# Two-step expert kernel on one core: the low parts of state, velocity, shared and halt layer, and the residual sum of iteration one, on GpSimd instead of VectorE

## What is computed

```python
v = 0; integrated = x
for _ in range(2):
    ctx = concat(integrated, v)
    shared_ctrl = gelu(ctx @ w_s1 + b_s1) @ w_s2 + b_s2
    x_shared, v_shared = _inl(shared_ctrl, integrated, v, mu)   # alpha, beta, gate
    hidden = gelu(ctx @ w1[expert] + b1[expert])                # the two experts of the token
    ctrl = hidden @ w2[expert] + b2[expert]
    x_r, v_r = _inl(ctrl, integrated, v, mu), weighted over the two
    x_next = sw * x_shared + (1 - sw) * x_r
    v_next = sw * v_shared + (1 - sw) * v_r
    halt = sigmoid(gelu(x_next @ w_h1 + b_h1) @ w_h2 + b_h2)
    refined = gelu(x_next @ w_f1 + b_f1) @ w_f2 + b_f2
    integrated = integrated + halt * refined * integration_weight
    v = v_next
```

## Time and profile before

| | before |
|---|---|
| median of 3 runs | 372.2 us (371.07 to 373.6) |
| the profiled execution | 371.76 us, of it 370.0 us span |
| TensorE busy | 332.4 us (90%) |
| VectorE busy | 285.4 us (77%) |
| ScalarE busy | 196.3 us (53%) |
| GpSimd busy | 17.4 us (5%) |
| mean granted TensorE clock | 0.967 |

### The profile page before, as it was taken

One profiled execution on the slowest core, in us unless ns is written; L12 is line 12 of the kernel. 1 busy time (PEld: TensorE's weight loads), 2 busy tenths in 40 slices (PEclk: granted clock), 3 DMA queues, 4 the chain that ended last, 5 costly groups with the idle time before them and its releaser, 6 DMA issues.

```text
span 370.0 us, 4365 instructions
## 1 busy us (share of the span) xinstructions
PE 332.4 (90%) x1508; PEld 229.5 (62%) x1516; DVE 285.4 (77%) x596; ACT 196.3 (53%) x306; POOL 17.4 (5%) x20
## 2 busy tenths in 40 slices
PE   4989999899897696897999999999999999989943
PEld 4754985454565474575765776767767767756621
DVE  0648676565968769989889999999989988991942
ACT  3500053477372682468586866748467366356421
POOL 0030111211111102000000000000000000000000
PEclk9989999999999999699899999999999999999985
DMA  7999910000000000000000000000000000000000
GB/s 264 424 411 293 357 41 0 1 1 2 0 2 1 0 2 0 0 2 1 1 2 0 0 0 2 0 2 1 0 3 0 0 0 30 0 0 30 28 1 28
DMA packets 10725, 17.84 MB, mean 48 GB/s; under 512 B 336, under 2 KB 8528, under 8 KB 9424
## 3 DMA queue, kind: packets, MB, share of 16 engines
q1 hardware_dynamic: 10704, 17.57, 13.7%
HBM read 16.52 MB, written 1.05 MB: 47 GB/s over the span
## 4 chain that ended last, share of the span: by engine, by line
PE 70%; DVE 14%; issue 8%; ACT 3%; POOL 2%; DMA 2%; POOLq 1%; ACTq 0%; SPq 0%; DVEq 0%
PE ps L1124 66%; DVE zz L761 3%; DVE lst L746 2%; POOL lrs L347 2%; DMA ctxT<-in_ctxT 2%; PE ps L1221 1%; PE ps L1200 1%; ACT hid L467 1%; DVE st L646 1%; DVE lmv L749 1%; PE ps L1307 1%; DVE a L662 1%; POOLq L62 1%; PE ps L1295 0%; DVE lve L751 0%
## 5 line engine op out<-in xcount | busy, mean ns | idle before, releaser
L1124 PE MATMUL ps<-hm_odd,ew_hi 128*128 128x512 f32 (+1 forms) x169 | 52.6, 423 | 0.0
L1124 PE MATMUL ps<-hm_even,ew_hi 128*128 128x512 f32 (+1 forms) x160 | 49.2, 415 | 0.0
L1124 PEld LDWEIGHTS ps<-hm_odd,ew_hi 128*128 128x128 f32 (+1 forms) x169 | 28.4, 192 | 5.9
L1124 PEld LDWEIGHTS ps<-hm_even,ew_hi 128*128 128x128 f32 (+1 forms) x160 | 26.4, 189 | 5.1
L1124 PE MATMUL ps<-hm_odd,ew_lo 128*128 128x512 f32 (+1 forms) x80 | 27.8, 398 | 0.0
L1124 PE MATMUL ps<-hm_even,ew_lo 128*128 128x512 f32 (+1 forms) x80 | 27.4, 391 | 0.0
L467 ACT ACTIVATE hid<-ps,pB 128x512 f32<-128x512 f32 x32 | 21.7, 687 | 10.6 <-PE ps L1124 9.9
L1124 PE MATMUL ps<-x_hi,w1x_hi 128*128 128x512 f32 x40 | 19.9, 498 | 5.6 <-ACT hid L467 3.9
L761 DVE TENSOR_SCALAR zz<-ps,lmv,lrs 128x128 f32<-128x128 f32 x48 | 16.4, 405 | 7.7 <-POOL lrs L347 7.5
L855 DVE SCALAR_TENSOR_TENSOR ring<-ring,pB,hid 128x1024 f32<-128x1024 bf16 x16 | 20.5, 1282 | 0.9
L746 DVE BATCH_NORM_STATS2 lst<-ps 128x6 f32<-128x128 f32 x48 | 10.7, 286 | 11.9 <-PE ps L1200 11.8
(11 more groups left out here) (271 smaller groups left out, 750.4 us busy)
## 6 DMA issues: line engine op xcount, KB each, us to landing
ring<-in_fc1b SPq DMA_DIRECT2D x4, 1024.0 KB, 17.3
ring<-in_fc2a SPq DMA_DIRECT2D x4, 1024.0 KB, 9.9
packC<-in_packC SPq DMA_DIRECT2D x1, 1152.0 KB, 9.2
pB<-in_packB SPq DMA_DIRECT2D x1, 1109.5 KB, 10.0
ctxT<-in_ctxT SPq DMA_DIRECT2D x2, 512.0 KB, 6.4
xtok<-in_xtok SPq DMA_DIRECT2D x1, 1024.0 KB, 9.0
xT<-in_xT SPq DMA_DIRECT2D x1, 1024.0 KB, 11.0
a<-in_fc1a SPq DMA_DIRECT2D x1, 1024.0 KB, 13.0
```

The lines of the kernel that those rows point to most:

```text
L1124: return pe.matmul(out, lhsT, rhs, start=start, stop=stop)
```

## The change

Four pieces of VectorE's work move to GpSimd. `shared_low` is `shared_halves`, `state_low` is the part of `state_split` for steps 2 to 7 (for steps 0 and 1 the split stays on VectorE), `residual` is line 1081, and `halt_low` moves under its own name for steps 0 to 6; VectorE keeps its own `halt_low` and calls it once, for step 7. In numbers: 8 instructions on `hsh`, 6 on `x_lo`, 4 on `v_lo`, 4 on `xT` and 7 on `h1s`. VectorE's final sum now waits for GpSimd's residual (`xsum`). On GpSimd each of the new instructions is followed by a wait for its own semaphore.

```diff
--- before.py
+++ after.py
@@ -346,6 +346,51 @@
                 pool.wait_ge(sem("lve"), n + 1)
                 pool.tensor_tensor(lrs[:, n % 2, :], lve[:, n % 2, :], mhalf[:, 0:BPC], ALU.pow)\
                     .then_inc(sem("lrs"), 1)
+
+            def shared_low(s):
+
+                pool.wait_ge(sem("hs"), s + 1)
+                pool.wait_ge(sem("hsu"), s + 1)
+                pool.tensor_tensor(hsh[64:128, s % 2, :], hs[64:128, :], hsh[64:128, s % 2, :].bitcast(F),
+                                   ALU.subtract).then_inc(sem("hsl"), 1)
+                pool.wait_ge(sem("hsl"), s + 1)
+
+            def state_low(s):
+
+                c = s % NCH
+                pool.wait_ge(sem("hid_ps"), 5 * s)
+                pool.wait_ge(sem("xhi"), s + 1)
+                pool.tensor_tensor(x_lo, xi[:, ck(c)], x_hi.bitcast(F), ALU.subtract).then_inc(sem("xlo"), 1)
+                pool.wait_ge(sem("xlo"), s + 1)
+                if s >= NCH:
+                    pool.wait_ge(sem("vhi"), c + 1)
+                    pool.tensor_tensor(v_lo, vT[:, ck(c)], v_hi.bitcast(F), ALU.subtract).then_inc(sem("vlo"), 1)
+                    pool.wait_ge(sem("vlo"), c + 1)
+
+            def residual(s):
+
+                pool.wait_ge(sem("xi"), s + 1)
+                pool.tensor_tensor(xT[:, ck(s)], xT[:, ck(s)], xi[:, ck(s)], ALU.add).then_inc(sem("xsum"), 1)
+                pool.wait_ge(sem("xsum"), s + 1)
+
+            def halt_low(s):
+
+                pool.wait_ge(sem("h1"), s + 1)
+                pool.tensor_tensor(h1s[32:64, :], h1[32:64, :], h1s[32:64, :].bitcast(F), ALU.subtract)\
+                    .then_inc(sem("h1lo"), 1)
+                pool.wait_ge(sem("h1lo"), s + 1)
+
+            pool.wait_ge(sem("lrs"), 3 * NCH)
+            shared_low(0)
+            for s in range(STEPS):
+                if s + 1 < STEPS:
+                    shared_low(s + 1)
+                if 2 <= s < NCH + 2:
+                    residual(s - 2)
+                if s + 2 < STEPS:
+                    state_low(s + 2)
+                if s >= 1:
+                    halt_low(s - 1)
 
         @block.scalar
         def _(act):
@@ -881,35 +926,21 @@
                 c = s % NCH
                 if s >= 1:
                     dve.wait_ge(sem("hid_ps"), 5 * s)
-                if s < 2:
-                    dve.tensor_copy(x_hi, xi[:, ck(c)]).then_inc(sem("xhi"), 1)
+                dve.tensor_copy(x_hi, xi[:, ck(c)]).then_inc(sem("xhi"), 1)
                 dve.wait_ge(sem("xhi"), s + 1)
                 dve.tensor_tensor(x_lo, xi[:, ck(c)], x_hi.bitcast(F), ALU.subtract).then_inc(sem("xlo"), 1)
-                if s >= NCH:
-                    dve.wait_ge(sem("vhi"), c + 1)
-                    dve.tensor_tensor(v_lo, vT[:, ck(c)], v_hi.bitcast(F), ALU.subtract).then_inc(sem("vlo"), 1)
-
-            def hidden_masked(s, next_state):
+
+            def hidden_masked(s):
 
                 kept(s, 1)
                 if s == 1:
                     weigh(NCH - 2, 2)
                 kept(s, 2)
-                if next_state:
-                    state_split(s + 1)
                 lower(s, 0)
                 lower(s, 1)
                 kept(s, 3)
                 lower(s, 2)
-                shared_halves(s)
                 lower(s, 3)
-
-            def shared_halves(s):
-
-                dve.wait_ge(sem("hs"), s + 1)
-                dve.wait_ge(sem("hsu"), s + 1)
-                dve.tensor_tensor(hsh[64:128, s % 2, :], hs[64:128, :], hsh[64:128, s % 2, :].bitcast(F),
-                                  ALU.subtract).then_inc(sem("hsl"), 1)
 
             ln_stats("ffn", 0)
             ln_scale("ffn", 0)
@@ -1013,7 +1044,6 @@
             kept(0, 3)
             state_split(1)
             lower(0, 2)
-            shared_halves(0)
             lower(0, 3)
             route(NCH - 1)
             dve.wait_ge(sem("consts"), 4)
@@ -1077,9 +1107,8 @@
                 link(dve.scalar_tensor_tensor(rr, th, 1.0, rr, ALU.add, ALU.mult))
                 if s < NCH:
                     dve.tensor_tensor(xi[:, ck(c)], xi[:, ck(c)], rr, ALU.add).then_inc(sem("xi"), 1)
-                    dve.wait_ge(sem("xi"), s + 1)
-                    link(dve.tensor_tensor(xT[:, ck(c)], xT[:, ck(c)], xi[:, ck(c)], ALU.add))
                 else:
+                    dve.wait_ge(sem("xsum"), c + 1)
                     dve.tensor_tensor(res[:, ck(c)], xT[:, ck(c)], rr, ALU.add).then_inc(sem("res"), 1)
 
             def state_next_split(s):
@@ -1105,9 +1134,7 @@
                 if s >= 1:
                     state_next_split(s - 1)
                 if s + 1 < STEPS:
-                    hidden_masked(s + 1, s + 2 < STEPS)
-                if s >= 1:
-                    halt_low(s - 1)
+                    hidden_masked(s + 1)
                 if s == 0:
                     slot_masks(NCH - 1)
             stepped(STEPS - 1)
```

## The result

The changed kernel takes 376.0 us (median of four executions, 375.2 to 377.0) against 372.5 us (371.1 to 373.6) for the kernel before on the same chip: a ratio of 1.0088, with a 95% interval of 1.0065 to 1.0111. It is slower by 3.5 us; 379.3 was forecast. The profiled execution took 375.86 us (span 374.1); the one of before took 371.76 (span 370.0).

The account below looks back on a forecast made before the run. VectorE was taken to pace iterations 2 to 4; holds of 1.15 us, each replacing 0.69, summed to +7.06 us on 371.76 (378.8), plus half a microsecond for the clock: 379.3 us, range 370.0 to 387.

Parts of the forecast that it names:

- VectorE paces iterations 2 to 4: Step loop: TensorE waits for VectorE's `xn_lo`, so each moved instruction's effect on VectorE's time repeats in the kernel's time.
- GpSimd holds VectorE back: Shared SBUF path: a two-input GpSimd instruction keeps VectorE's next two-input or fast copy instruction out; chance 0.63 for at least 0.97 us.
- the rival without a hold: VectorE is not held and gets 3.45 us shorter per iteration; kernel 1.8 us faster, near 370.0 us; chance 0.18.
- The hold of 1.15 us: Each moved instruction blocks VectorE for GpSimd's assumed duration, 1.15 us, and saves 0.69: d = +0.46 us each.
- s = 2, 3, 4 late by 1.85 (2.2 less the slack of 0.36), 4.5 and 6.8 us: Hand-over of `xn_lo` to TensorE: VectorE late by +2.2, +4.5 and +6.8 us, TensorE's slack of 0.36 at s = 2.
- the formula 17d - 1.0: Lateness at s = 4 for any net cost d per moved instruction: seventeen instructions less pauses; 3.7 us for a 0.97 us hold.
- s = 5 and 6 absorb the rest: VectorE is 7.8 and 7.3 us late, but TensorE's slack of 1.0 and 1.6 us keeps it at +6.8.
- s = 7, +0.26 us more: At s = 7 VectorE loses two instructions (-1.38) and meets one hold (+1.15); TensorE was waiting, so +7.06 after +6.8.
- Tail 0: After s = 7: last `h1s` stays on VectorE; the one before comes some 0.6 us later, but hidden: 0.
- +0.5 us for TensorE's clock, between 0 and 1.7: Behind TensorE's stall at s = 4: a lower granted clock could cost up to 1.7 us; half a microsecond was added.
- GpSimd's order: GpSimd's strict queue: no TensorE wait expected for `h1s` or `x_lo`; a first one would add less than 1 us.
- Signs: If right: VectorE instructions beside GpSimd's take 1.8 us; s = 3 starts near 233, s = 4 near 259, idle 2 or more.

Follow-up runs that it names:

- the 18 early instructions: Of the change's 29 instructions only the 18 that GpSimd executes up to s = 4 move, the rest stay on VectorE: 377.5 us against 372.6, ratio 1.014.
- the 11 late ones: Only the other 11 of the change's instructions, from `x_lo` of step 6 on, go to GpSimd: 372.8 us, ratio 1.0007.
- The extra two-input instructions: Kernel before kept whole, plus 29 unused GpSimd subtractions of 512 columns, two SBUF inputs, where the moved ones run: 394.8 us against 372.7, ratio 1.059.
- the one-input experiment: Kernel before kept whole, plus 29 unused GpSimd copies of 512 columns with one SBUF input: 378.8 us against 372.7, ratio 1.016.
- the one with the changed kernel's split ahead: Changed kernel with VectorE's split into `xn_hi` and `xn_lo` placed ahead of `refine`, `xn_hi` in its own place: 375.3 us, ratio 1.0075.
- the deferred sums: Kernel before with the split ahead of `refine` and the four residual sums deferred to iterations 5 and 6, all on VectorE: 370.7 us, ratio 0.995.

## Why the prediction was right or wrong, point by point

- **VectorE paces iterations 2 to 4: right.** TensorE's new waits are where they were put (0.78, 1.77 and 1.85 us), all loss is made by the 18 early instructions (377.5 us against 372.8 for the 11 late ones), and an earlier `xn_lo` only moves the wait elsewhere.
- **GpSimd holds VectorE back: right.** The extra two-input instructions, whose result nobody reads, cost 22 us; the rival without a hold (370.0 us) is out. The row that decided, GpSimd's 0.97 us of waiting at 139.98, had its mirror image in `xn_lo`. (Of line 855 1.11 us were left at that moment and not 0.97; nothing hangs on it.)
- **The hold of 1.15 us: the term that failed.** It was set equal to GpSimd's own duration, and that was put between two reads one after the other (0.95) and two reads and a write (1.37). Both steps were off. The instruction alone takes 1.26 us and not 1.15, and it holds VectorE for less than it lasts: 0.95 us on `xn_lo`, 0.98 over an iteration. The rate of the earlier trace rows gives 0.95 for two reads as well, but as far as the runs show that is chance: one read would by it be half of that, and 0.28 to 0.33 us was measured. The prediction had a better value in hand: for 0.97 us, the one wait between the two engines then on record, it gives 3.7 us at s = 4. By the estimate from the Trainium skill that the prediction named (GPSIMD Engine Reference, "Elementwise — side-by-side cycle accounting", 1.12 us) it would have been wrong by nearly as much: the hold was 0.98 us. (With 1.12 the sum comes out 0.8 us lower by its own list, 27 times 0.03, and not 0.5.)
- **s = 2, 3, 4 late by 1.85 (2.2 less the slack of 0.36), 4.5 and 6.8 us: measured 1.05, 2.95 and 4.52 at equal clock.** The pattern was right, the steps were not. How late VectorE is, step by step, in the kernel with the early instructions only (its timeline of VectorE against that of before):

| stretch | forecast | measured |
|---|---|---|
| to the first gate of stepped(1) | +0.6 | +0.11 |
| from there to the end of `xn_lo` at s = 2 | +1.61 | +1.30 |
| to `xn_lo` at s = 3 | +2.3 | +1.55 |
| to `xn_lo` at s = 4 | +2.3 | +1.56 |
| together | 6.8 | 4.52 |

  The last three rows are the hold: twelve of them, of 0.98 us instead of 1.15. The first row is a second, smaller failure: five holds were charged there, less two pauses. But of GpSimd's six instructions up to then only three lengthen one of VectorE's, and two of the others, at 157.44 and 191.54, lie wholly or mostly in VectorE's pauses, which have grown, since work has left. VectorE was not late there but early, and waited for ScalarE's gates. Timelines of VectorE, first before, then in the kernel with the early ones:

```profile
193.99 1.23 DVE L1047 TENSOR_TENSOR kv<-kv,hB 128x1024 f32<-128x1024 f32 x1 [0.82 <-ACT kv L578]
...
194.10 1.22 DVE L1098 TENSOR_TENSOR kv<-kv,hB 128x1024 f32<-128x1024 f32 x1 [2.22 <-ACT kv L627]
```

  This is also why the formula 17d - 1.0 gives too little with the measured hold (3.9 us with d = 0.29): it lets VectorE come early at stepped(1), by 5 x 0.29 - 1.7 = -0.25 us, where ScalarE does not allow it (+0.11), and d is 1.56/5 = 0.31.
- **s = 5 and 6 absorb the rest: right.** The changed kernel has no wait there, and counted from the last layer norm TensorE is 3.26, 3.28 and 3.25 us late at s = 4, 5 and 6, although GpSimd's instructions hold VectorE at s = 5 as well (`xn_lo` 1.67 us).
- **s = 7, +0.26 us more: not so.** VectorE gains there: `hsh` and `h1s` are gone from its row, TensorE's wait falls from 1.52 to 0.96 us, and 0.56 us comes back.
- **Tail 0: right.** The `h1s` of step 6 does arrive late, as this row of the changed kernel's timeline of TensorE shows, and the delay is hidden: the last `refine_a` starts 4.23 us later than before, the one at s = 7 4.20.

```profile
346.74 1.95 PE L1151 MATMUL ps<-zz,pB 128*128 128x512 f32 x4 [0.75 <-POOL h1s L379]
```

- **+0.5 us for TensorE's clock, between 0 and 1.7: not needed here, but both ends exist.** The changed kernel's busy time behind its two stalls:

```profile
231.80:236.00 4.20, 4.15 (x21) 2.95 (x22) 4.20 (x2) 4.16 (x5) 3.25 (x2) 1.00 0.00 0
...
257.00:262.00 5.00, 4.93 (x24) 3.59 (x25) 5.00 (x4) 4.96 (x6) 3.26 (x2) 1.00 0.02 5
```

  The clock stays at 1.00. In the one-input experiment and in the one with the changed kernel's split ahead it fell to 0.57 and 0.59 behind stalls only 0.1 to 0.2 us longer, but stayed full behind another one of about the same length in each.
- **The sum.** The forecast was 379.3 us and 376.0 was measured, 3.3 less. Too much in it were 2.3 us up to s = 4 (6.8 against 4.52; 1.8 of it the hold, 0.5 the lateness at stepped(1)), 0.5 for the clock and 0.26 + 0.56 = 0.8 at s = 7: 3.6 together. The rest, 0.3, is within the spread of the changed kernel's executions (375.2 to 377.0).
- **GpSimd's order: right.** Apart from that `h1s`, nobody waits for a moved instruction; they take up to 2.2 us each and fit.
- **Signs.** Instructions that ran beside GpSimd's took 1.64 us and 2.31 us; s = 3 was put near 233 and s = 4 near 259, they came at 231.85 and 257.07, each after a wait of 1.8 us where 2 or more was named.

## What to carry to other kernels

An elementwise instruction with two inputs in SBUF that is moved from VectorE to GpSimd is not off VectorE: here it gave back 0.69 us and took 0.95 to 0.98 us of whichever VectorE instruction it met. Where VectorE had no pause the move lost time (ratio 1.014 for 18 instructions), and where it had pauses it neither lost nor gained (1.0007 for 11). If a hold of about that size is on record, take it rather than a duration built up from rates. To relieve an engine that paces a stretch, move the work in time (the deferred sums: 1.7 us gained) and look at the distance of one landmark from iteration to iteration, since a wait that is removed at one hand-over comes back at the next one. To price such a hold, keep the kernel whole and add the instruction with its result unused.

## What the runs showed of the hardware that I had not expected

- The hold is shorter than the instruction: 0.95 to 0.99 us of 1.26 (two inputs, 512 columns), 0.41 to 0.44 of 0.73 (two inputs, 256), 0.28 to 0.33 of 0.61 (one input, 512). Two inputs cost three times one input, not twice.
- A GpSimd instruction that only writes (512 columns, 0.53 us) leaves VectorE's two-input subtraction at 0.69 us but stretches a single-input cast from 0.43 to 0.83.
- GpSimd gets its turn between two VectorE instructions that stand back to back: `x_lo` and `v_lo`, at 231.28 and 232.98, each delayed one line 900 by 1.03 us.
- The same TensorE stall of 1.97 or 1.98 us in one kernel was followed once by a full clock and once by 0.57; the stall of 2.65 us at about 171 to 175 us was followed by 0.79 in the profile of before and by 1.00 in that of after (174 to 182 us). An outcome of this kind moves a single execution by 1 to 2 us, about half of what the change itself does.
